# Folding attention weights three heads in two steps of an experts' loop, with the context's masks moved up behind them

## The reference

```
x = x + tanh(g_xattn[0]) * L0_xattn(layernorm(x), ctx)    # 16 heads of 16, query and key normed
x = x + tanh(g_ffn[0])   * L0_ffn(layernorm(x))           # 16 experts, 8 per token, and a shared one
x = x + tanh(g_xattn[1]) * L1_xattn(layernorm(x), ctx, mask)   # 16 heads of 128, 8 key/value heads
x = x + tanh(g_ffn[1])   * L1_ffn(layernorm(x))           # ternary weights, silu(up) * gate

# an expert e of L0_ffn, for all tokens, in the latent space of 64
ye  = (xl @ rw1[e].T) * square(relu(xl @ rwg[e].T)) @ rw2[e].T
acc = acc + w_dense[:, e:e+1] * ye

# second attention, head h
q = x Wq[h];  k = ctx Wk[h // 2];  v = ctx Wv[h // 2]
out += softmax(q k^T / sqrt(128) + mask) v Wo[h]
```

## Time and profile before

| | us |
|---|---|
| median of 3 executions (lowest, highest) | 1515.71 (1512.38, 1518.31) |
| the profiled execution | 1514.76 |
| its span in the trace | 1513.5 |
| mean granted TensorE clock, share of full | 0.958 |
| busy PE / DVE / ACT / POOL, share of the span | 90% / 68% / 59% / 45% |

### The profile page before, as it was taken

How to read it: one execution, slowest core, us unless ns; L and a number is a source line. 1 busy time by engine, 2 the same in 40 slices (tenths; PEclk the granted TensorE clock), 3 DMA queues, 4 the chain that set the end, 5 groups by cost and what they waited for, 6 DMA issues and landing times.

```text
span 1513.5 us, 24828 instructions
## 1 busy us (share of the span) xinstructions
PE 1359.0 (90%) x8430; PEld 680.1 (45%) x8524; DVE 1024.0 (68%) x2259; ACT 899.1 (59%) x1575; POOL 680.9 (45%) x753
## 2 busy tenths in 40 slices
PE   5688696888997888789999989999999999999998
PEld 4243242434433244234555545555555555555555
DVE  6676477587797445756676666765667776767657
ACT  4756454657774665556565666555665555656554
POOL 4035153244003013226665546665576655555553
PEclk8798798999998999889999999999999999999999
DMA  4000210301132010010000000000010000000000
GB/s 171 1 1 3 48 41 2 66 2 33 36 119 79 2 57 1 6 44 23 7 1 2 0 23 23 7 1 23 1 28 1 29 25 5 27 3 2 1 1 28
DMA packets 20485, 36.66 MB, mean 24 GB/s; under 512 B 4899, under 2 KB 15239, under 8 KB 19335
## 3 DMA queue, kind: packets, MB, share of 16 engines
q1 hardware_dynamic: 20358, 35.07, 8.0%
HBM read 26.53 MB, written 1.15 MB: 18 GB/s over the span
## 4 chain that ended last, share of the span: by engine, by line
PE 48%; issue 3%; DVE 2%; ACT 2%; POOL 2%; another core or an unknown queue 0%; DVEq 0%; POOLq 0%; ACTq 0%
PE BK L724 48%; POOL arena L2133 1%; DVE arena L1688 1%; DVE arena L2322 0%; ACT arena L1973 0%; ACT arena L1985 0%; DVE arena L2328 0%; POOL arena L1096 0%; PE BK L1369 0%; ACT L1016 0%; PE BK L1043 0%; ACT arena L2354 0%; ACT arena L2358 0%; POOL arena L2124 0%; POOL arena L1094 0%
## 5 line engine op out<-in xcount | busy, mean ns | idle before, releaser
L724 PE MATMUL BK<-arena 128*128 128x512 bf16 (+12 forms) x8100 | 1314.1, 364 | 109.2 <-DVE arena L1525 20.0
L724 PEld LDWEIGHTS BK<-arena 128*128 128x128 bf16 (+7 forms) x8194 | 643.6, 110 | 750.0 <-issue 185.4
L2133 POOL TENSOR_TENSOR arena<-arena 128x512 bf16<-128x512 f32 (+1 forms) x416 | 440.1, 1062 | 243.3 <-ACT arena L1973 185.8
L1973 ACT ACTIVATE arena<-BK,arena 128x512 f32<-128x512 f32 (+1 forms) x416 | 285.5, 687 | 198.7 <-PE BK L724 187.7
L1525 DVE TENSOR_REDUCE arena<-BK 128x1 f32<-128x512 f32 x384 | 240.5, 681 | 79.2 <-PE BK L724 78.7
L1871 ACT ACTIVATE arena<-BK 128x512 f32<-128x512 f32 (+1 forms) x416 | 225.5, 594 | 112.2 <-PE BK L724 104.2
L1713 DVE TENSOR_TENSOR BK<-BK,arena 128x512 f32<-128x512 f32 (+1 forms) x352 | 244.1, 693 | 44.6 <-ACT arena L1973 40.6
L1688 DVE CUSTOM_DVE_ANT_0 arena<-BK,arena 128x512 bf16<-128x512 f32 (+1 forms) x256 | 147.0, 574 | 109.0 <-PE BK L724 106.3
L1985 ACT ACTIVATE arena<-BK 128x512 bf16<-128x512 f32 (+1 forms) x256 | 129.8, 507 | 104.2 <-PE BK L724 103.2
L1727 DVE SCALAR_TENSOR_TENSOR arena<-BK,arena 128x256 f32<-128x256 f32 x128 | 56.1, 479 | 34.9 <-PE BK L724 34.8
L2036 POOL TENSOR_TENSOR arena<-arena 128x1024 f32<-128x1024 f32 (+2 forms) x15 | 23.2, 1550 | 83.7 <-DVE arena L1467 83.7
(11 more groups left out here) (184 smaller groups left out, 852.7 us busy)
## 6 DMA issues: line engine op xcount, KB each, us to landing
arena<-arena SPq DMA_DIRECT2D x144, 50.0 KB, 2.2
arena<-in_ctxT SPq DMA_DIRECT2D x8, 800.5 KB, 4.4
arena<-in_ctxk SPq DMA_DIRECT2D x4, 768.0 KB
arena<-in_wo SPq DMA_DIRECT2D x1, 2048.0 KB, 8.7
arena<-in_wqT SPq DMA_DIRECT2D x1, 2048.0 KB, 7.5
arena<-in_x SPq DMA_DIRECT2D x4, 256.0 KB, 9.7
arena<-in_rsel SPq DMA_DIRECT2D x1, 1024.0 KB, 9.3
arena<-in_rw1T SPq DMA_DIRECT2D x1, 1024.0 KB, 5.5
```

What stands on the lines that cost most here:

```text
L724: return T.matmul(out_, lhsT, rhs, start=start, stop=stop, skip_group_check=True)
L1973: A.activation(P1[k][0:m, :], BK[i][0:m, :], ACT.Exp, scale=SCALE1, bias=mcb[0:m, b, kt:kt + 1]).then_inc(free[i], 1)
L2133: G.tensor_tensor(Pl[k][0:m, :], P1[k][0:m, :], Ph[k][0:m, :], ALU.subtract).then_inc(p_low, 1)
```

## The change

In odd steps from 3 to 15 the loop takes two pieces of `work` in place of one.

```
--- before
+++ after
@@ -459,6 +459,8 @@
                     piece("ac", p // E)
             if s >= 3:
                 next(work, None)
+                if s < 16 and s % 2:
+                    next(work, None)
                 if s == 24:
                     piece("l1set")
             if s >= 31:
```

## The result

The changed kernel takes 1517.03 us (median of 20 executions, 1515.26 to 1518.61); the kernel before, run beside it, 1513.95 us (median of 20, 1512.37 to 1518.31). The medians are 3.1 us apart. The ratio is 1.0018, 95% interval 1.0011 to 1.0025, so between 1.7 and 3.8 us slower: clear of noise, and well inside the 0.5% that the prediction counts as no change. The profiled execution of the changed kernel took 1517.81 us with a span of 1516.5, against 1514.76 and 1513.5, so the two profiled executions differ by 3.05. The mean granted clock rose from 0.958 to 0.961.

A forecast was written before the change was run, and what follows sets the result against it. PE's own work was taken to set the pace in steps 3 to 17, DVE to be busier in the mask stretch. 9.4 + 1.35 - 4.8 - 2.3 = +3.65 us, giving a median of 1519.4 us, range 1510 to 1526.

The forecast's parts named there:

- Part A: Steps 3 to 11: five second heads each wait for BK7's release and add 1.88 us, together 9.4 us.
- Part B: Step 13's head copy to step 20's relu: context chain on DVE and ACT -0.3, clock fall +1.65, together +1.35 us.
- Part C: Relu of step 20 to that of step 27: without masks on DVE, -4.8 us.
- Part D: Relu of step 27 to that of step 30: POOL's mask differences over, full clock, -2.3 us.
- The root of step 26 waiting under 2 us: Sign in the changed profile, late steps: the root, which waited 6.56 us behind masks, would wait under 2 us.
- Masks hide: Last rival: PE goes on beside the context's work up to step 20's relu; -6.2 us, 1509.5 us; chance 0.10.
- Late steps give nothing back: Rival: steps 20 to 27 held by the relu, square, products, norm chain; +8.4 us, 1524.1 us; chance 0.18.
- The clock falls again later: Rival: clock falls twice before step 20's relu and again in steps 27 to 30; +6.7 us, 1522.4 us; chance 0.14.
- From step 30 on the rest shifts as it stands: Behind the relu of step 30 both kernels' lists are the same, so the rest was taken to shift unchanged.

The follow-up runs named there:

- heads_only: Changed kernel with heads packed as in the change but the context's pieces left in steps 19 to 26: 1517.92 us, ratio 1.0024 to the kernel before.
- cy_apart: Changed kernel with the second `cy` cast moved behind step 16's relu and square, the context ending a step later: 1516.55 us, ratio 1.0011 to the kernel before.
- split_dn: Changed kernel with each pair's first head ahead of `dn`, the second behind it, in steps 3 to 11: 1521.23 us, ratio 1.0042 to the kernel before.
- one_piece: Changed kernel with pairs in steps 3 to 11 and one piece a step from step 12: 1517.07 us, ratio 1.0019 to the kernel before.
- late_pairs: Changed kernel with pairs only in steps 11, 13 and 15, `dn` between their heads: 1511.36 us, ratio 0.9980 to the kernel before.
- late_pairs_adjacent: Changed kernel with pairs only in steps 11, 13 and 15, both heads behind `dn`: 1513.74 us, ratio 0.9996 to the kernel before.

## Why the prediction was right

It said 1519.4 us, no measurable change, a little to the slow side; measured was 1517.03. Of the 2.4 us between, 1.8 is the median of before, which over 20 executions is 1513.95 and not the 1515.71 of the three that were shown. The sum of +3.65 stands against +3.68 in the stage, +3.05 between the profiled executions and +3.08 between the medians. A, C and D came out term by term. That B did so too, and with it the sum to some hundredths, is luck, as said below.

- **Part A, right.** 9.42 against 9.4, and again 9.42 in heads_only. The price of a second head (two copies, wake-up, the head) held in all five steps; relu to relu they are 1.80 to 1.89 longer. The copies stand 1.86 and 1.88 apart, where a first load ahead of the wait would have made it some 1.72. The rule of the Trainium skill (TensorE: Matmul & The Clock Gate, section "Architectural detail") on loads pulled ahead gives nothing at such a release: in step 11 the second head's first load starts at 591.98 and its first matmul at 591.99, both after it; the row of before was the better guide.
- **Part B, right in sum by luck: two misses cancel.** Without the clock the path to PE's resumption at the `tl` was taken as 18.9 after the last copy and took 18.17. The term mis-sized is the chain to the relu of step 16, 9.45 against 8.70: the second `cz` took 1.10 us, not 1.48, step 14's product came 0.2 sooner, and from the cast's start to the relu it was 0.66, not 0.79. Its mechanism, the cast ahead of the relu, is shown by cy_apart. Then the clock: "it falls once here, 3.3 us at half, 1.65 lost". It fell once, but for 6.8 us, and from PE's resumption to the relu of step 20 it took 4.99 where 1.07 + 1.65 = 2.72 had been counted: 2.27 lost within B, 0.6 more than the 1.65 it had been given. The first `mk` took 1.61 us where it had taken 0.97 before, beside two POOL differences; it cost nothing, since the product behind it waited another 0.44 for ACT.
- **Part C, right.** -4.73 against -4.8, and the marks inside fit: relu of step 22 at 5.92 (5.9 predicted), of step 23 at 10.00 (9.95), of step 26 at 15.96 (15.9). heads_only shows the cause by bringing the 24.77 back.
- **Part D, right.** -2.28 against -2.3, at full clock throughout. The 1.4 of it that the prediction puts down to the clock hung on that: with one fall in D, split_dn and cy_apart get back 1.1 and 1.2 in all.
- **A sign that was set wrong.** "The root of step 26 waiting under 2 us": it waits 2.62. The prediction's own chain gives that (relu at 15.9, square done at 17.2, root at 19.75), and the bound was not worked out from it.
- **A slip in the range.** It was to take in all the rivals' times, but the last rival's, 1509.5, lies below its end of 1510.
- **The rivals.** Masks hide: no, PE waits 3.06 us for the `tl`. Late steps give nothing back: no, by heads_only. The clock falls again later: not in this kernel, but it does in cy_apart (C and D 3.2 us longer than in the changed kernel), in one_piece (2.65 us longer) and in D of split_dn (1.15 longer), so a chance of 0.14 was not too high.
- **Not foreseen.** "From step 30 on the rest shifts as it stands": the second attention came out 1.4 us shorter, by a clock fall that is no longer there.
- **The clock.** The fall in steps 27 to 30 is gone; from 620 to 636 PE had been 56% busy ahead of it and is 85% busy now. The one behind a wait for the `tl` stayed (605.4 before, behind a wait of 1.86; 616.0 now, behind 3.06) and is twice as long. That fits the rule of the Trainium skill (TensorE: Matmul & The Clock Gate, section "What's actually happening") that the low clock is the default state and activity releases the throttle. Two runs speak against reading it as a sure forecast: in one_piece the same list of instructions lost the clock in step 3 and here it did not, and in cy_apart PE waited 3.19 us for the `tl` and kept it.

## What to carry to other kernels

Before putting two pieces that share a bank into one step, look at what stands between their releases: here the second costs 1.88 us side by side and 0.88 with an independent piece between, but only where that piece does not already cover another wait. When a busy engine's work is moved out of a late stretch, follow it to its new place and add up both chains to the next common mark; the two sides here were 10.7 and 7.0, and only their small difference is the result. Two or three pairs, in steps where the cover was free, turned the stage's +3.7 us into -4.6 and -4.1. The cover is the smaller part of that: three pairs side by side, without it, already made it -2.8 (by the medians 0.7 us under before, and 3.0 with the cover), since three second heads cost less than five and the late steps still lose most of the masks.

## What the runs showed of the hardware

- **The same instructions, with and without a fall of the clock.** Around 892 us the clock falls to half in the kernel before and not in the changed one, after a stretch with PE 56% and 58% busy; the difference is 1.38 us. In late_pairs PE is busy for only 1.68 of the 4 us from 888 to 892, and the clock stays full up to 896. In step 3 one_piece falls and the change doesn't, with one list, for 1.2 us. Between these executions the work reaches the place at another time; whether that is what decides was not tried and stays open.
- **Gains in front of a clock fall are partly given back.** cy_apart gained 4.86 us up to step 20 and lost 3.2 behind it, 2.9 of them in two steps with the clock at half; late_pairs's 3.0 us over late_pairs_adjacent shrank to 1.3 in the profiled stages. A fall need not cost anything: the one in part C of heads_only, 3.4 us long, cost none, since DVE set the time there. Executions of one kernel differ by the clock as well: late_pairs_adjacent took 1511.06 us at a mean clock of 0.962 and 1515.89 at 0.957.
- **DVE beside POOL.** With both operands in SBUF and POOL differences at work, the first mask sum took 1.61 us against 0.97 alone, `cz` 1.10 and 1.48 against 0.85, and POOL's own two differences 2.22 in place of 1.61. The products, which have an operand in PSUM, took 0.69 in both cases. How much an operation loses doesn't follow from how long the two overlap: the `cz` of 1.48 ran beside POOL for about 0.8 us, the one of 1.10 for its whole length.
